# First cross-attention of a two-layer decoder: the turn of the maxima moved ahead of a unit's last turned block, and the short plain key block split over the two row halves

## The reference

```python
q_big = apply_rope(einsum('bshk,hkq->bshq', q_hk, w_kc_q))
kv_r  = apply_rope(kv_c)                          # (4, 1601, 64)
q_r   = einsum('bshq,hqr->bhsr', q_big, W_qr)
k_r   = einsum('bld,hdr->bhlr', kv_r, W_kr)
scores = einsum('bhsr,bhlr->bhsl', q_r, k_r)      # per batch and head 256 x 1601
attn  = softmax(scores, axis=-1)
ctx_c = einsum('bhsl,bld->bhsd', attn, kv_r)
```

## Time and profile before

| | |
|---|---|
| median of 3 runs | 1361.86 us (1356.94 to 1368.56) |
| span of the profiled execution | 1379.6 us (no other time of that execution is listed) |
| TensorE busy | 1272.7 us, 92% |
| VectorE, ScalarE, GpSimd busy | 868.2, 634.6, 824.0 us |
| stage of the 32 units | about 214 to 737 us |

### The profile page before, as it was taken

One profiled execution on the slowest core, in us unless ns is written; L12 is line 12 of the kernel. 1 busy time (PEld: TensorE's weight loads), 2 busy tenths in 40 slices (PEclk: granted clock), 3 DMA queues, 4 the chain that ended last, 5 costly groups with the idle time before them and its releaser, 6 DMA issues.

```text
span 1379.6 us, 20358 instructions
## 1 busy us (share of the span) xinstructions
PE 1272.7 (92%) x7123; PEld 826.8 (60%) x7123; DVE 868.2 (63%) x1490; ACT 634.6 (46%) x1687; POOL 824.0 (60%) x748
## 2 busy tenths in 40 slices
PE   7999997999999999999999758998999999989792
PEld 4865554666666666666668643445776874556582
DVE  4756666677777777778865636675666123664443
ACT  3731123445554455544551416887665115872151
POOL 1267005799999999999993445887444004560444
PEclk9999997999999999999999888999999997998897
DMA  9501111000000000000005620000000105200263
GB/s 261 134 9 32 37 31 27 9 8 9 9 11 10 9 9 9 10 11 9 9 5 176 195 65 2 1 1 1 1 1 1 27 1 155 63 1 32 69 142 118
DMA packets 66172, 58.91 MB, mean 43 GB/s; under 512 B 19424, under 2 KB 62968, under 8 KB 65560
## 3 DMA queue, kind: packets, MB, share of 16 engines
q1 hardware_dynamic: 62952, 49.09, 12.7%
q0 software_dynamic: 3120, 8.52, 2.6%
HBM read 40.69 MB, written 8.52 MB: 36 GB/s over the span
## 4 chain that ended last, share of the span: by engine, by line
PE 79%; DVE 6%; ACT 5%; POOL 4%; issue 4%; DMA 1%; DVEq 0%; SPq 0%; POOLq 0%; ACTq 0%
PE PS L515 73%; PE PS L523 5%; ACT s_sc L1402 2%; POOL a_m L2137 2%; POOL a_m L2131 2%; DVE s_mx L1859 1%; ACT a_m L1356 1%; DVE pm L1622 1%; DVE HN L1504 0%; PE PS L729 0%; DMA f_xg<-token_rows,f_ids 0%; POOL s_sc L2152 0%; PE PS L685 0%; POOL f_xg L2119 0%; PE PS L623 0%
## 5 line engine op out<-in xcount | busy, mean ns | idle before, releaser
L2080 POOL TENSOR_TENSOR PWS<-PWS 128x1024 f32<-128x1024 f32 x160 | 379.7, 2373 | 45.1 <-ACT PWS L1286 25.8
L1622 DVE TENSOR_REDUCE pm<-PS 128x2 f32<-128x1024 f32 x192 | 225.8, 1218 | 69.3 <-PE PS L515 68.7
L1286 ACT ACTIVATE PWS<-PS 128x512 f32<-128x512 f32 (+1 forms) x416 | 213.3, 599 | 78.4 <-PE PS L515 78.2
L515 PE MATMUL PS<-PWS,KVR 128*64 128x256 f32 (+1 forms) x1664 | 185.8, 380 | 0.0
L515 PE MATMUL PS<-QALL,KH 128*128 128x512 f32 (+1 forms) x416 | 182.6, 439 | 0.9 <-DVE QM L1646 0.9
L515 PE MATMUL PS<-QM,KL 68*128 68x512 f32 (+1 forms) x416 | 167.3, 402 | 0.0
L2152 POOL TENSOR_SCALAR s_sc<-s_sc,s_ri 128x128 f32<-128x128 f32 (+1 forms) x256 | 104.5, 429 | 98.9 <-DVE s_ri L1866 98.9
L515 PEld LDWEIGHTS PS<-PWS,KVR 128*64 128x64 f32 (+1 forms) x1664 | 121.4, 137 | 59.0 <-issue 0.9
L515 PEld LDWEIGHTS PS<-QALL,KH 128*128 128x128 f32 (+1 forms) x416 | 77.9, 187 | 76.9 <-ACT PWS L1286 57.4
L1402 ACT ACTIVATE s_sc<-PS,s_nb 128x128 f32<-128x128 f32 (+1 forms) x256 | 104.5, 433 | 3.9 <-DVE s_nb L1862 3.9
L1859 DVE TENSOR_REDUCE s_mx<-PS 128x2 f32<-128x512 f32 (+2 forms) x112 | 65.7, 611 | 50.1 <-PE PS L515 50.0
(11 more groups left out here) (328 smaller groups left out, 2518.3 us busy)
## 6 DMA issues: line engine op xcount, KB each, us to landing
QALL<-qlo SPq DMA_DIRECT2D x32, 128.0 KB, 2.4
QM<-QALL SPq DMA_DIRECT2D x64, 64.0 KB, 2.0
f_w<-in_L_ffn_w_dram SPq DMA_DIRECT2D x2, 2048.0 KB
tile_results<-e_y SPq DMA_DIRECT2D x31, 128.0 KB
a_nat<-in_L_attn_w_qkv_dram SPq DMA_DIRECT2D x1, 3072.0 KB, 13.0
x_wq<-in_L_xattn_Wq_dram SPq DMA_DIRECT2D x1, 2048.0 KB, 10.4
x_wo<-in_L_xattn_Wo_dram SPq DMA_DIRECT2D x2, 1024.0 KB, 6.9
a_wo<-in_L_attn_w_o_dram SPq DMA_DIRECT2D x1, 2048.0 KB, 17.5
```

Of the source, the lines that this page charges most:

```text
L515: return nc.tensor.matmul(o, a, b, start=start, stop=stop, **kw)
L1286: nc.scalar.activation(PW[c][0:rows, j * HALF:(j + 1) * HALF], st_bank("block", LT * u + lt)[0:rows, :], ACT.Exp).then_inc(p_ready, 1)
L1622: V.tensor_reduce(pm[u % 2][:, :, i // 3, i % 3], src, AX, ALU.max).then_inc(nat_read, 1)
L2080: G.tensor_tensor(ACC[:, :], PW[0][:, :] if i == 0 else ACC[:, :], PW[i + 1][:, :], ALU.add).then_inc(acc_step, 1)
```

## The change

Three things are changed, all in this stage.

The tail of a unit is computed as the plain scores are: each head from its own 64 rows, the two heads in two banks, its place in the ring of three and `CTX_BANK`. TensorE waits for the last tail's reduction and for the last context to be moved out before it writes there, and the context waits for the tail's reduction. VectorE reduces the two banks by two instructions.

The turned blocks of a unit are listed in three parts instead of two: 0 to 5, 6 to 11, and 12 alone. From unit 1 on, the turn of the next unit's maxima (and of keys, where there are any) stands ahead of block 12, and the two late plain scores behind it. The ring's order follows.

VectorE spreads the maxima (`maximum_rows`) ahead of the late reductions, from unit 1 to unit 30.

```diff
-        FRONT, BACK = range(0, 6), range(6, LT)
+        FRONT, BACK, LAST = range(0, 6), range(6, LT - 1), range(LT - 1, LT)
...
             ST_ITEMS += [("block", LT * u + lt) for lt in (BACK if u else ())]
             ST_ITEMS += [("maxima", u + 1)] if u + 1 < UNITS else []
             ST_ITEMS += [("keys", *keys_due(u))] if keys_due(u) else []
+            ST_ITEMS += [("block", LT * u + lt) for lt in (LAST if u else ())]
             ST_ITEMS += [("sums", u - 1)] if u else []
...
-                ps = st_begin("tail", u)
+                both = (st_begin("tail", u), CTX_BANK)
...
-                for h in range(2):
-                    for st in range(2):
-                        a = h * 256 + st * P
-                        last = mm(ps[:, a:a + 66], QALL[:, p, b, h, st * P:(st + 1) * P], KH[b % 2][:, 3 * HALF:3 * HALF + 66])
+                if u >= 1:
+                    pe.wait_ge(tail_read, u)
+                if u >= 2:
+                    pe.wait_ge(ctx_read, u - 1)
+                for st in range(2):
+                    for h, ps in enumerate(both):
+                        rows = slice(h * D, (h + 1) * D)
+                        last = mm(ps[:, st * P:st * P + 66], QALL[rows, p, b, h, st * P:(st + 1) * P],
+                                  KH[b % 2][rows, 3 * HALF:3 * HALF + 66])
                 last.then_inc(tail_full, 1)
...
                 if u > 0:
                     turned_scores(u, BACK)
-                for n in late:
-                    plain_scores(n)
+                else:
+                    for n in late:
+                        plain_scores(n)
                 if u + 1 < UNITS:
                     turn_maxima(u + 1)
                 if keys_due(u):
                     keys(*keys_due(u))
+                if u > 0:
+                    turned_scores(u, LAST)
+                    for n in late:
+                        plain_scores(n)
                 if u >= 1:
                     weight_sums(u - 1)
...
-                src = st_bank("tail", u).rearrange("p (h s c) -> p h s c", h=2, s=2)[:, :, :, 0:LREST]
-                V.tensor_reduce(pm[u % 2][:, :, :, 3], src, AX, ALU.max).then_inc(tail_read, 1)
+                for h, bank in enumerate((st_bank("tail", u), CTX_BANK)):
+                    src = bank[:, 0:2 * P].rearrange("p (s c) -> p s c", s=2)[:, :, 0:LREST]
+                    ins = V.tensor_reduce(pm[u % 2][:, h, :, 3], src, AX, ALU.max)
+                ins.then_inc(tail_read, 1)
...
                 if u + 1 < UNITS:
                     all_maxima(u + 1)
+                if 0 < u < UNITS - 1:
+                    maximum_rows(u + 1)
                 for n in late:
                     maxima(n)
-                if u + 1 < UNITS:
-                    maximum_rows(u + 1)
+                if u == 0:
+                    maximum_rows(1)
```

More of the change, by code:

```diff
@@ L456, in decoder @@
         for u in range(UNITS):
-            ST_ITEMS += [("block", LT * u + lt) for lt in (FRONT if u else range(LT))]
+            ST_ITEMS += [("block", LT * u + lt) for lt in (FRONT if u else range(0, LT))]
             ST_ITEMS += [("tail", u + 1)] if u + 1 < UNITS else []
@@ L745, in context @@
                 b = u // PAIRS
+                pe.wait_ge(tail_read, min(u + 2, UNITS))
                 if u >= 1:
@@ L776, in _ @@
                     turned_scores(0, BACK)
+                    turned_scores(0, LAST)
                     for n in range(PLAINS + 2, PLAINS + AHEAD):
@@ L1304, in _ @@
                 weights(u, BACK)
+                weights(u, LAST)
                 if keys_due(u):
```

## The result

The changed kernel took 1376.55 us (median of 6 runs, 1367.83 to 1382.66), the kernel before 1365.21 us beside it (6 runs, 1356.94 to 1370.59): ratio 1.0092, 95% interval 1.0055 to 1.0129. So it is slower by 11.3 us, where 5.5 were forecast, and the time lies just above the range. It is 9.2 us above the forecast time, 1367.4: 5.8 of these are the larger difference, and 3.4 are the kernel before, whose median rose from 1361.86 to 1365.21 us with three more runs.

What follows compares the result with a forecast made beforehand. TensorE's path through each unit was taken as the bound in units 1 to 30. Terms 10.8 - 5.1 + 0.3 - 0.5 = +5.5 us on the median 1361.86 gave 1367.4 us, range 1353 to 1376.

Steps and rivals of the forecast that it cites:

- The tail's term: Short plain block split into two pairs over 64 rows: 0.17 us saved a unit, 5.1 us for units 1 to 30.
- The ring's terms: Turn takes one of three banks, delaying block 12: 0.32 us lost in 18 units, 0.36 in eight, 0.73 in three.
- the free turn: Rival at the turn: block 12 does not move; a gain of 8.0 us, to 1353.9; chance 0.12.
- The halves did overlap: Rival at the tail: half loads do not overlap, costing 0.05 us a unit; +12.1 us, 1374.0; chance 0.14.
- VectorE did not hold the turn: Rival at the turn: it waits for VectorE's maxima; 1 us late in all units costs +15, 1382; chance 0.04.
- no gain for 66 columns: Tail, by the skill's advice: the split brings nothing, a loss of 0.05 us instead of the gain, 6.6 us in total.
- The 0.5 us of the last batch: Last batch: spreading the maxima earlier mostly stops VectorE holding up the middle plain scores; -0.5 us taken.
- the 0.3 of VectorE's second read: Unit 0 and ahead of it, where VectorE is the bound: the second tail reduction costs twice 0.17, +0.3 us.
- I carry the difference to the median: Whole run: the +5.5 us worked out on the profile is added to the median, 1361.86, giving 1367.4 us.
- nothing outside the stage is touched: Rest of the program, outside the first cross-attention: a change there would have to be chance.
- +5.5: Sum of the terms in the first cross-attention: 10.8 - 5.1 + 0.3 - 0.5 us, a small loss that may not show.
- the 17.7: Whole run: the profiled execution's span, 1379.6 us, lies 17.7 us above the median of three runs.

Runs made afterwards that it cites:

- the first set: The changed kernel, unedited, in its first six runs beside the kernel before: 1376.55 us, ratio 1.0092, mean clock 0.9552.

## Why the prediction was wrong

**What held.** The tail's term, 0.17 a unit, is what every unit outside the last batch shows, and alone it gives its gain on the chip. The ring's terms, 0.32, 0.36 and 0.73, measured 0.31, 0.35 and 0.71; taking the turn off the ring gave them back and more. Of the rivals, the free turn did not happen (ScalarE ended the wait of block 12, at 3.50 us), but it is what comes out when the turn needs no bank of the ring: it was priced at 8.0 us gained, and that kernel's stage gained 7.56. The halves did overlap. VectorE did not hold the turn: it waited for it.

The Trainium skill, "TensorEngine Tiling (Array Packing)", section "Instruction Overhead", advises against a tiling factor from a dimension that is already small. The prediction read this as no gain for 66 columns, and that did not come: tail to next block 1.15 to 0.88 us, of which 0.10 is paid back ahead of the tail. The split takes its factor from the 128 rows, not from the 66 columns, so these runs contradict the prediction's reading rather than the advice. The 0.10 agrees with its section "Key Properties", by which a change of the tiling mode drains the engine: 0.33 us from a turned block to 64-row work, 0.23 to 128-row work; that the 0.10 is a drain, no row shows.

**What was off in size.** The 0.5 us of the last batch did not come, and the 0.3 of VectorE's second read ahead of unit 1 is not seen: the first block of unit 1 starts at 246.56 us, 0.26 earlier than before, but that start scatters by 6.4 us in one kernel, so nothing can be read from it. The two terms nearly cancel in the sum.

**The step that failed** is "I carry the difference to the median", with its ground, "nothing outside the stage is touched", and a range that was made of the stage's terms alone. It failed in both of its parts. The median was that of three runs: with six it is 3.4 us higher, more than a third of the 9.2 us by which the forecast is missed. And the difference of the whole run is not that of the stage. The stage's was right (+5.33 for +5.5), and its place too. But the 900 us ahead of it and behind it are not a constant that is added: their time goes with the clock that TensorE is granted there, and the changed kernel's clock is lower by 0.0042 on average (0.9562, 0.9604), which at 8.75 us for 0.01 is 3.7 us; in the first set, at 0.9552, it is 4.6. With 5.3 that makes 9.9 of the 11.3 us. The rest, 1.4, is left open: 0.9604 stands in for the clock of six runs of before that is not listed, and by chance alone such a set can lie 0.002 off, 1.7 us. Over its four sets the changed kernel is 9.8 us above before in the mean (1374.0 and 1364.2): 5.3 by the stage, 3.7 by the clock, 0.8 unaccounted for. The profile of before showed the warning: a span 17.7 us above the median, with 0.92 behind the stage. The text named the 17.7 and drew no range from it; it also named 13.6 us as what a measurement cannot tell from no change, while its range ended 8.6 us above its forecast. That the time fell 0.6 us outside the range, and not inside, is little more than chance.

**What stays open.** Why a program gets 0.951 or 0.961 is not settled, nor whether the changed order has any part in it. It isn't the time of arrival alone, and not the order of the stage by itself; with ten extra matmuls, which nobody reads, it is 0.9611, with twenty 0.9512. The standard error of a set's mean is 0.001 to 0.002, so single rows of the table can be off by that, and their order among themselves is not to be read closely.

## What to carry to other kernels

An instruction that is moved into a wait also brings the buffer it writes: where a short ring sets the waits, count which reader each later item now needs, and put the moved one into a place outside the ring if there is one. That the turn of the maxima was free in itself could be seen only with its bank taken away. And a difference of a few microseconds in one stage should be read at full clock in that stage, while the whole run's median carries the clock of all other stages: ask how far the mean clock moves the time before a range is given, take the base from more than three runs, and list the clock beside every time.

## What the runs showed of the hardware that was not expected

- Executions of one program differ in the mean granted clock of TensorE, 0.945 to 0.966 in 32 runs of the changed kernel and 0.950 to 0.968 in 117 of before, and 0.01 of it goes with 8.8 us of 1364 here. Units 1 to 30 of the first cross-attention have 1.00, the 2.4 GHz level, in every profile shown; ahead of them and behind them the clock is a mix with 1.2 GHz, 0.94 to 0.97 and 0.91 to 0.94. One stretch of 304 matmuls took 33.4 us in one execution and 44.5 in another.
- Programs differ in their mean: sets lie from 0.9512 to 0.9617, though behind the stage they are the same program; the five sets of the kernel before lie between 0.9600 and 0.9612.
- The step from a turned block to 64-row work costs 0.10 us more than the one to 128-row work (0.33 and 0.23), and eight 64-row loads take the 0.52 us of four 128-row ones.
